# Other places for the last four units' rows of W in the setup of a two-step matrix product kernel

## The reference

```python
w = weights[subjects]
cond = jnp.einsum('bct,bcd->bdt', x, w)
result = jnp.einsum('bnd,od->bno', cond, W_base) + b_base
logits = jnp.einsum('bnd,ed->bne', cond, W_gate)
probs = jax.nn.softmax(logits)
top_p, top_i = jax.lax.top_k(probs, 2)      # then divided by their sum
route_w = (jax.nn.one_hot(top_i, E) * top_p[..., None]).sum(-2)
h = jnp.einsum('bnd,erd->bner', cond, A) * route_w[..., None]
return x + result + jnp.einsum('bner,eor->bno', h, B) * SCALING
```

## Time and profile before

| what | us |
|---|---|
| median of 3 runs | 1578.59 (1575.66 to 1580.38) |
| the profiled execution, device time | 1579.12 |
| its span in the trace | 1577.3 |
| TensorE busy in the span | 1506.0 (95%) |
| VectorE busy | 1352.3 (86%) |
| ScalarE, GpSimd busy | 626.1 (40%), 640.5 (41%) |

### The profile page before, as it was taken

The page is one execution under the profiler, slowest core; times in us unless marked ns, Lnnn a source line. Parts: engine busy times, 40 slices in busy tenths (PEclk is TensorE's granted clock), DMA queues, the critical chain, the costliest instruction groups (busy, mean ns, idle before and its releaser), DMA issues.

```text
span 1577.3 us, 25817 instructions
## 1 busy us (share of the span) xinstructions
PE 1506.0 (95%) x9411; PEld 808.5 (51%) x9411; DVE 1352.3 (86%) x2257; ACT 626.1 (40%) x1026; POOL 640.5 (41%) x508
## 2 busy tenths in 40 slices
PE   4678999999999999999989999999999999999998
PEld 4554554555455555555545455555455555455553
DVE  6788999999899999999968888888888888888875
ACT  6864444444543445434413332223332323332321
POOL 2565555666665555665522122122122122122122
PEclk9899999999999999999999999999999999999999
DMA  6234555655555555655797333344333344433342
GB/s 232 94 132 156 163 165 173 191 166 161 150 176 167 161 168 178 177 179 157 227 339 247 108 123 101 99 141 126 116 121 91 111 141 123 118 116 94 114 111 74
DMA packets 169567, 235.95 MB, mean 150 GB/s; under 512 B 71898, under 2 KB 88794, under 8 KB 167130
## 3 DMA queue, kind: packets, MB, share of 16 engines
q1 hardware_dynamic: 167426, 219.63, 46.0%
q10 hardware_dynamic: 2016, 14.68, 2.4%
HBM read 147.83 MB, written 86.43 MB: 149 GB/s over the span
## 4 chain that ended last, share of the span: by engine, by line
PE 73%; DVE 11%; issue 4%; POOL 2%; DMA 1%; ACT 1%; SPq 0%; DVEq 0%; ACTq 0%; POOLq 0%
PE bank_x L1427 8%; PE bank_x L1429 8%; PE bank_x L1428 8%; PE bank_y L1427 8%; PE bank_y L1429 8%; PE bank_y L1428 8%; PE bank_z L1427 3%; PE bank_z L1429 3%; PE bank_z L1428 3%; PE bank_h L1427 2%; PE bank_h L1429 2%; PE bank_h L1428 2%; PE bank_c L1427 2%; DVE t_sums L1070 2%; PE bank_c L1429 2%
## 5 line engine op out<-in xcount | busy, mean ns | idle before, releaser
L602 POOL TENSOR_TENSOR x_res<-x_res,t_sums 128x512 f32<-128x512 f32 x255 | 350.5, 1377 | 843.4 <-DVE t_sums L1075 684.1
L1427 PE MATMUL bank_y<-TT,s_parts 128*128 128x512 f16 x768 | 292.1, 380 | 4.7 <-DVE TT L1185 4.2
L1427 PE MATMUL bank_x<-TT,s_parts 128*128 128x512 f16 x768 | 292.9, 381 | 1.3 <-DVE TT L1185 1.3
L1428 PE MATMUL bank_x<-TT,s_parts 128*128 128x512 f16 x768 | 292.5, 381 | 0.0
L1429 PE MATMUL bank_x<-TT,s_parts 128*128 128x512 f16 x768 | 292.3, 381 | 0.0
L1429 PE MATMUL bank_y<-TT,s_parts 128*128 128x512 f16 x768 | 291.9, 380 | 0.0
L1428 PE MATMUL bank_y<-TT,s_parts 128*128 128x512 f16 x768 | 291.9, 380 | 0.0
L710 ACT ACTIVATE p_copies<-bank_x,y_inv 128x512 f32<-128x512 f32 x128 | 87.7, 685 | 417.7 <-PE bank_x L1429 307.3
L1075 DVE TENSOR_TENSOR t_sums<-t_sums,inv_w 128x512 f32<-128x512 f32 x255 | 233.8, 917 | 8.7
L1045 DVE TENSOR_TENSOR s_parts<-a_full,s_parts 128x512 f16<-128x512 f32 x224 | 192.9, 878 | 33.0 <-ACT s_parts L695 33.0
L574 POOL TENSOR_TENSOR x_res<-x_res,BT 128x512 f32<-128x512 f32 x128 | 206.9, 1616 | 26.3 <-DMA x_res<-in_x_dram 23.3
(11 more groups left out here) (243 smaller groups left out, 2750.5 us busy)
## 6 DMA issues: line engine op xcount, KB each, us to landing
x<-in_x_dram SPq DMA_DIRECT2D x32, 1024.0 KB, 5.8
x_res<-in_x_dram SPq DMA_DIRECT2D x128, 256.0 KB, 4.0
part_scratch<-x_res SPq DMA_DIRECT2D x128, 256.0 KB, 3.0
x_res<-part_scratch SPq DMA_DIRECT2D x128, 256.0 KB, 3.9
out_dram<-x_res SPq DMA_DIRECT2D x128, 256.0 KB, 3.0
wt_scratch<-late_words SPq DMA_DIRECT2D x64, 224.0 KB, 3.4
TT<-wt_scratch ACTq DMA_DIRECT2D x14, 1024.0 KB, 8.3
x_parts<-in_L_ffn_W_base_dram SPq DMA_DIRECT2D x18, 512.0 KB, 6.4
```

Source lines behind the costliest of these rows:

```text
L602: nc.gpsimd.tensor_tensor(XR[:, xr_slot(m), :], XR[:, xr_slot(m), :], TM[:, m % 2, :], ALU.add).then_inc(r_added, 1)
L1427: nc.tensor.matmul(dst, lhs[0], rhs[0], start=start, stop=False, skip_group_check=chained)
L1428: nc.tensor.matmul(dst, lhs[0], rhs[1], start=False, stop=False, skip_group_check=chained)
```

## The change

No instruction of an engine is added or removed; places, semaphores and orders change.

- **Places.** Unit 5's rows go into `bias` (before: `a_full`), unit 6's into `X` (before: `x_parts`), unit 7's stay in `a_full`. Unit 7 gets two semaphores of its own.
- **SyncE.** `load_rows(5)` goes where the bias load stood, `load_rows(7)` where `load_rows(5)` stood, `load_rows(6)` waits for unit 4 (`w_tr` 20) instead of for the store of the features. The bias is loaded after unit 5 is read out (`w_tr` 24), and `load_x(1)` after unit 6 (`w_tr` 28; before after unit 4, 20).
- **GpSimd.** `w_lower(4)` and `w_lower(5)` come first, and then two pairs of `add_bias` and `add_r`, ahead of `w_lower(6)`.
- **ScalarE.** `sum_rows(5)`, (6) and (7) each come earlier, and the two halves of `w_upper(7)` stand together, ahead of `split_x_hi(1, ...)`.
- **VectorE and TensorE.** `find_maxima(1)` moves from before `w_scales(6)` to behind `w_first_sum(7)`, `find_top(1)` from behind `w_other_sums(6)` to behind `w_other_sums(7)`; `transpose_maxima(1)` moves from ahead of `w_quads(7)` to behind it.

```diff
         def rows_of(g, i):
             if g < NU // 2:
                 return early_rows[(2 * g + i) % 4]
-            return (X, af_rows, xp_rows, af_rows)[g - NU // 2][:, i, :]
+            if g == NU // 2 + 1:
+                return bias[:, i * KH:(i + 1) * KH]
+            return (X, None, X, af_rows)[g - NU // 2][:, i, :]
...
-                    at = (2 * g + i) % 4 + 4 * (g // (NU // 2))
+                    at = 8 + i if g == NU - 1 else (2 * g + i) % 4 + 4 * (g // (NU // 2))
...
             sp.wait_ge(w_tr, 4 * (NU // 2))
-            sp.dma_start(bias, b_base.rearrange("(a o) -> a o", a=1).to_broadcast([P, O])).then_inc(bias_in, 16)
+            load_rows(5)
             for m in range(2, 4):
                 load_tile(m)
             sp.wait_ge(s_lo, NPROD)
-            load_rows(5)
+            load_rows(7)
             sp.wait_ge(b_lo, 1)
             sp.dma_start(bt_dram, BT_first).then_inc(bt_out, 16)
+            sp.wait_ge(w_tr, 4 * 5)
+            load_rows(6)
             sp.wait_ge(f_lo, 2)
             sp.dma_start(ft_dram, FT_second.rearrange("p f s n -> p (f s n)")).then_inc(ft_out, 16)
-            sp.wait_ge(w_tr, 4 * 5)
+            sp.wait_ge(w_tr, 4 * 6)
+            sp.dma_start(bias, b_base.rearrange("(a o) -> a o", a=1).to_broadcast([P, O])).then_inc(bias_in, 16)
+            sp.wait_ge(w_tr, 4 * 7)
             load_x(1)
-            sp.wait_ge(ft_out, 16)
-            load_rows(6)
             store_tile(0)
-            sp.wait_ge(w_tr, 4 * 6)
-            load_rows(7)
...
+            w_lower(4)
+            w_lower(5)
             pool.wait_ge(bias_in, 16)
             add_bias(0)
+            add_r(0)
             add_bias(1)
-            w_lower(4)
-            add_r(0)
+            add_r(1)
+            w_lower(6)
             add_bias(2)
-            w_lower(5)
-            add_r(1)
             add_bias(3)
-            w_lower(6)
...
             split_f_hi(1, FT_second)
+            sum_rows(5)
             w_upper_first(4)
             copy_p(0, 0, P5_COPY)
-            sum_rows(5)
             w_upper_rest(4)
+            sum_rows(6)
             copy_p(0, 0, U2_COPY)
             copy_p(0, 0, P4_COPY)
             w_upper_first(5)
-            sum_rows(6)
+            sum_rows(7)
             w_upper_rest(5)
-            sum_rows(7)
             w_upper(6)
-            w_upper_first(7)
+            w_upper(7)
+            act.wait_ge(ft_out, 16)
             split_x_hi(1, 0)
             split_x_hi(1, 1)
-            w_upper_rest(7)
...
             w_first_sum(5)
-            find_maxima(1)
             w_scales(6)
             w_other_sums(5)
             finish(0, 0, C12)
             w_first_sum(6)
             w_scales(7)
             w_other_sums(6)
-            find_top(1)
             finish(0, 0, C21)
             finish(0, 0, C22)
             w_first_sum(7)
+            find_maxima(1)
+            w_other_sums(7)
+            find_top(1)
             scale_x(1)
-            w_other_sums(7)
...
             pe.wait_ge(f_full, 2)
+            w_quads(7)
             transpose_maxima(1)
-            w_quads(7)
             spread_maxima(1)
             pe.wait_ge(f_lo, 1)
             pe.wait_ge(w_inv, NU)
```

More of the change, by code:

```diff
@@ L223, in adaln_ffn_kernel @@
         wc_in = sem("wc_in")
-        stage_in = [sem(f"stage{i}_in") for i in range(8)]
+        stage_in = [sem(f"stage{i}_in") for i in range(10)]
         a_in = sem("a_in")
@@ L715, in sum_rows @@
                 for i in range(2):
-                    at = (2 * g + i) % 4 + 4 * (g // (NU // 2))
-                    act.wait_ge(stage_in[at], 16 * (g % (NU // 2) // 2 + 1))
+                    at = 8 + i if g == NU - 1 else (2 * g + i) % 4 + 4 * (g // (NU // 2))
+                    act.wait_ge(stage_in[at], 16 if g == NU - 1 else 16 * (g % (NU // 2) // 2 + 1))
                     junk_at = ((B22, B11) if g >= NU // 2 else (B11, T1))[i]
```

## The result

The changed kernel takes 1584.76 us (median of 8 runs, 1582.19 to 1586.6); the kernel before took 1579.28 us beside it (8 runs, 1575.66 to 1580.94). The ratio is 1.0035, with a 95% interval of 1.0024 to 1.0046: 5.5 us more (3.8 to 7.3). That is inside the range and just past the 0.3% bound, so it belongs to the case that had 0.16, "slower, by the same ports in more places" (1584.2 us), and not to the likeliest one (1582.0 us). The interval does not clear that bound, and the median is 0.2 us inside the range's upper end of 1585.0. The profiled execution has a span of 1583.2 us, against 1577.3.

The account below looks back on a forecast made before the run. TensorE was taken as the bound from about 120 us, VectorE's list before it. The list ending at 117.3 plus 0.1 + 2.9 + 2.6 + 2.0 gave 124.9 against 121.5, so 1578.59 + 3.4 = 1582.0 us; range 1577.0 to 1585.0.

Parts of the forecast that it names:

- slower, by the same ports in more places: Slower rival: find_top(1) stretched 1.0 us, clock 0.5, unit 6's rows 0.7; mark 5.6 us later, 1584.2 us; chance 0.16.
- the likeliest one: Case with the mark 1.5 to 4.7 us later, holding the forecast of 1582.0 us; chance 0.60.
- the mark: Moment in setup when product(0, 1, 1) starts on TensorE at full clock: 121.5 us before, forecast 124.9, 3.4 us later.
- Unit 6's rows: Setup, ScalarE: rows land at 85.2 us and are summed at 87.3; TensorE starts unit 6 at 92.6 instead of 95.19.
- w_scales(7): VectorE's list: 4.3 us beside GpSimd's four additions, with 1.5 us as the other bound; ends at 103.3.
- C21, C22 and w_first_sum(7): VectorE's list behind w_other_sums(6): two tiles and unit 7's first sum take 4.7 us, ending at 111.0.
- find_maxima(1): VectorE's list from 111.0: takes 2.5 us and does not wait for x, which lands by 107.0.
- find_top(1): Last piece of VectorE's list: takes 0.8 us and ends at 117.3.
- Features, product, clock: TensorE behind find_top(1): 2.9 us of features, 2.6 of product(0, 1, 0), 2.0 for the lower clock.
- Behind the mark: TensorE's unbroken work afterwards: the mark's delay reaches the end unchanged; other idle times than before would show the prediction wrong.
- The first rival: GpSimd out of the way: w_scales(7) takes 1.5 us, mark 1.3 us earlier, 1577.3 us; 0.20 for 1.5 later to 1.3 earlier.
- The early gain: Rival: TensorE's lead at unit 6, 4.2 to 4.8 us when done, carries through to 1573.8 us; chance 0.04.

Follow-up runs that it names:

- b_late_maxima: Kernel before, with only the maxima moved to the change's places and w_upper(7) whole ahead of split_x_hi(1) on ScalarE: 1583.57 us, ratio 1.0030.
- a_pe: Changed kernel with make_features(0) and product(0, 1, 0) put ahead of transpose_maxima(1) and spread_maxima(1) on TensorE: 1581.16 us, ratio 1.0017.
- a_top_free: Changed kernel with w_lower(7) on GpSimd held back until find_top(1) is through: 1583.62 us, ratio 1.0029.
- b_rows_only: Kernel before with two SyncE queue edits: second part of background rows ahead of tile 4's store, x tiles 4 and 5 loaded before stores 2 and 3: 1580.46 us.
- a_warm: Changed kernel with 22 extra matmuls ahead of transpose_maxima(1) and 18 behind it, to keep TensorE busy: 1584.2 us, ratio 1.0025.
- a_scales_free: Changed kernel with GpSimd waiting, ahead of tile 0's bias, until unit 7's scales are spread: 1585.24 us, ratio 1.0032.

## Why the prediction was right or wrong

**The mechanism was right.** TensorE loses, because features and `product(0, 1, 0)` stand behind `find_top(1)`; b_late_maxima makes nearly all of the loss with this and the order on ScalarE that goes with it, and a_pe gives half of it back by undoing it. **The size was 2.4 us short**: 5.8 at the mark, for 3.4. By the steps, with 1.0 taken off the moments of after:

- *Unit 6's rows*: forecast summed at 87.3, measured 87.8, and `w_first_sum(5)` 0.5 us late at 90.3, as ScalarE stood 1.68 us for the second half of the rows. TensorE started unit 6 at 93.1, forecast 92.6. The half microsecond was regained: C12 took 1.9 (96.91 to 98.80), not 2.3, and `w_first_sum(6)` ended at 99.0, to the tenth as forecast.
- *w_scales(7)*: forecast 4.3, measured 5.1. The row chosen was the right one; the first small instruction and three of the four with 128x128 outputs were stretched. **0.8 us.** Each stretched instruction ended within 0.1 us of the end of one of GpSimd's: the one at 102.47 at 103.77, where the addition begun at 102.42 ended at 103.68. The trace agrees with what the Trainium skill says of the shared ports (SBUF — State Buffer, section Who interferes with whom) that the prediction drew on: 1.38 us with GpSimd held back, 5.08 beside it.
- *C21, C22 and w_first_sum(7)*: forecast 4.7, measured 5.2 (108.07 to 113.23). **0.5 us**. The visible part is the second instruction of C21, 1.60 us beside `w_lower(6)` where the kernel before had 0.91; that of C22 took 0.97, before 1.20.
- *find_maxima(1)*: 2.5, as forecast, and it did not wait for x, which had landed 5.4 us after its issue at 100.59.
- *find_top(1)*: forecast 0.8, measured 1.8 (118.74 to 120.57). **1.0 us.** The row for the 0.8 was a lucky one, as a_top_free and b_rows_only show above. This was the slower rival's first term, priced at 1.0 there, and left out of the sum because `w_lower(7)` and `find_top(1)` were put at 116 to 117 "for both". It should have been in the sum: a coincidence that the forecast's own times show is not a rival, it is a step.
- *Features, product, clock*: forecast 2.9 + 2.6 + 2.0 = 7.5, measured 7.57 (120.73 to 128.30). Right, and a_warm confirms the 2.0 as 2.1. The slower rival's 2.5 for the clock was too much.
- *Behind the mark* the unbroken stretch is as it was, nearly. TensorE is busy for 197.96 us of the 200 from 200 us on, 197.94 before. At the end of step 0 the wait for rows is 2.63 us, 2.64 before, and the mark's delay stands behind it unchanged. Two smaller things are not as they were, which the prediction had named as a sign against it, and they offset each other: the kernel before waits 1.56 us at 164.18 for the next step's condition weights, the changed one 0.23 at 170.97, but runs at 0.58 of the clock from 150 to 153 us.

These three terms, 0.8 + 0.5 + 1.0 = 2.3 us, are the miss. Two of them, and the visible part of the third, are one thing, GpSimd beside VectorE. I had it once in the sum and once in a rival, as if the two were independent; a_scales_free shows that they are less free than that, as GpSimd's work must lie beside something and its additions free the buffers that VectorE writes next.

**A reading of the kernel before was wrong.** The prediction says that VectorE works "nearly without a pause" from 89 to 120 us and has "hardly a gap to close". It had two gaps there, both waits for ScalarE's copies of a unit:

```profile
101.54 0.69 DVE L1197 TENSOR_TENSOR s_parts<-s_parts,bank_d 128x512 f32<-128x512 f32 x1 [1.12 <-ACT TT L738]
...
116.66 0.69 DVE L1205 TENSOR_TENSOR late_words<-bank_z,s_parts 128x512 f32<-128x512 f32 x1 [2.71 <-issue]
```

For the second the profile names no releaser; the code waits there for ScalarE's third copy of unit 7 (`w_first`), which ScalarE made at 116.00 to 116.57, behind `split_x_hi(1, ...)`. In the changed kernel VectorE has no gap from 91.33 to the end of `find_top(1)`. So the change closed 3.8 us of gaps and put `scale_x(1)`, 1.2 us, behind the list. Against this, `w_first_sum(5)` starts 1.3 us later than before, counted from unit 4, and the same instructions take 3.7 us more. VectorE's list therefore ended 48.48 us after unit 4 before (the end of `w_other_sums(7)`) and 48.39 after (the end of `find_top(1)`). With the list ending at the same moment, the 5.8 us at the mark are the features and the product that now stand behind it, 2.9 + 2.6, and 0.4 us by which the lower clock costs more. The forecast did not use the wrong reading, as it summed the new list piece by piece; that sum let the list end 2.4 us earlier than before.

**The slower rival** came nearest to the time, 1584.2, in part by luck. Of its three terms only `find_top(1)` came as it had it. Its 0.5 for the clock was not there and its 0.7 for the rows was 0.5 and regained; `w_scales(7)` and C21, which it left alone, made up for them.

**The first rival** (GpSimd out of the way, 1577.3 us): GpSimd was not out of the way, and where an experiment held it back beside `w_scales(7)` the time was that of the change. **The early gain** of 2.1 us at unit 6 was down to 0.1 us at unit 7, which starts 33.08 us after unit 4, 33.21 before.

## What to carry to other kernels

If an engine works through a list without a gap, look at what stands behind its last piece on the others: moving a piece to the end of that list costs the consumers' own time on top, even though the list ends no later than before. Price a coincidence of two engines that your own timeline shows in the sum and not beside it, and do not take the price of a small instruction from one execution in which it may have been lucky. And a lead gained at one place is a gain only as far as the next queue that issues in a fixed order: look for the DMA whose issue stands behind a store.

## What the runs showed of the hardware

- One VectorE instruction on a 4x4 tile took 0.22 us with GpSimd idle (a_top_free) and 1.17 us when it began together with one of GpSimd's with two inputs (119.40 and 119.39 us, in the changed kernel). It ended as that one did; the stretched time is that of the neighbour (1.15 us here), not in proportion to its own. Where it began 0.1 us before the neighbour went over to its next instruction, in the kernel before, it took 0.22.
- Of small instructions beside the same neighbour some are stretched and some not: 1.14 us for the first of `w_scales(7)`, 0.17 for the next two. The second began at 101.17, between an addition that ended at 101.12 and one that began at 101.19; the third, a reciprocal at 101.38, ran within that addition and was not held.
- The granted clock does not follow from the length of the last idle time alone. The wait of 2.64 us at 142.52 in the kernel before was followed by a clock of 1.00 from 143 to 146 us, that of 2.63 us at 149.31 in the changed one by 0.58 from 150 to 153 us.
- Of forty added matmuls in idle time the first 22 held the small matmul behind them by 0.5 us (a_warm: 116.58 us, 0.57 after VectorE's last maximum; 0.05 in the changed kernel), which nothing waited for, and the other 18 held nothing (0.05 us in both). The 2.9 us of work behind them took 2.1 us less.
